# A new slot order for a six-layer transformer kernel, with five slots between projection and last use

## The chip, the cores and the metric

The kernel runs on one core of one Trainium2 chip. The metric is device time in microseconds (us) of one execution, taken as the median over runs. Everything is fp32 except the three-term projections, which use fp32r halves, and a bf16 mask.

## The reference

`x` is (8 batches, 256 tokens, 128 features). A layer norm comes first, and from its result two branches are computed:

```
s = linear_attention(xn) with a 3-tap convolution, then Wp, bp      # small, done once ahead of the layers
for i in range(6):                                                   # the bulk
    q, k, v = shift_tokens(x) @ Wqkv[i]          # 16 heads of 64
    q, k = l2norm(q) * qs, l2norm(k) * ks, then rotary with a scale
    att = softmax(8 * q k^T) v                   # windows of 32, each sees itself and the window before
    x = att @ Wo[i] + x
    h = layernorm(x) * g + b
    a, gate = shift_tokens(h) @ W1[i] + b1       # 341 + 341
    x = (a * gelu(gate)) @ W2[i] + b2 + x
out = x_in + s * silu(x)
```

## The kernel before

A step is one batch of one layer, so there are 6 x 8 = 48 steps, called n. A step has four units j = 0..3, one for each pair of a head octet and a 128-token tile; unit u = 4n + j. All five engines run one software pipeline written out by hand: each engine has a `body(n)` with a loop over four slots, and in slot u it works on unit u and on older units and older batches. Order within an engine is the order of the lines; engines meet only through semaphores.

What happens to a unit u, and in which slot, before the change:

- TensorE projects q, k, v of unit u into the PSUM banks ps_q, ps_k, ps_v (three matmuls each) in slot u.
- VectorE multiplies ps_q and ps_k with the rotary tables (`rotate`, two instructions each, into qk and qk_rot); ScalarE squares them (`squares_of`), VectorE sums the squares (`sum_squares`), clamps; ScalarE takes Ln and Exp (`start_norms`); VectorE does three small Newton instructions. GpSimd adds the rotary halves (`add_halves`) and multiplies by the norms (`normalise`). All in slot u.
- TensorE transposes q and k (`turn_qk`, into ps_qs and ps_tk) in slot u+2, ScalarE copies them out (`keep_turned`), TensorE computes the scores in the same slot (`scores`, 65 matmuls into ps_qs), VectorE finds and subtracts the maximum, ScalarE takes Exp, VectorE sums and inverts (`sums`).
- GpSimd divides (`divide`), TensorE transposes the probabilities (`turn_p`, into ps_po), ScalarE copies them block-diagonally (`keep_p`, two instructions), TensorE multiplies with v (`values`, 32 matmuls), ScalarE copies the result (`keep_attention`) in slot u+3.

The batch's own work hangs in certain slots: the out projection in two halves (`out_projection`), the layer norm (`ln_mean`, `ln_variance`, `ln_spread`), the first FFN matmul in three parts (`ff_up`, each copied by `ff_copy`), `gelu` on ScalarE, the gate product on GpSimd (`ff_gate`), the second FFN matmul (`ff_down`, 12 matmuls). Gelu needs another activation table than Ln and Exp, so ScalarE loads a table twice in each step. `ff_down` of batch n-3 is in slot j = 2 of step n, into ps_f.

Three rules of buffers matter. `qk` has two buffers, so `rotate(u)` waits until unit u-2 is transposed (`wait(dve, (tq_done, tk_done)[i], u - 1)`). `project(u+1)` waits until the bank ps_q (ps_k) of unit u is read. ps_po holds transposed probabilities, then the attention result, so `turn_p` waits for the `keep_attention` before it.

The pipeline is filled by running the first steps with what isn't there left out (`live`), steps from LAG on are a hardware loop, and `drain()` on each engine ends it, with silu and the last sums of the output.

Of the kernel before, what the change touches and what calls it, by code (L numbers as in the profile page):

```python
# [28 lines left out]
P = 128  # L29
# [10 lines left out]
UNITS = 4  # L40
STEPS = DEPTH * BATCHES
LAG = 3
# [20 lines left out]
def build(nc, x, wq, wk, wv, wp, bp, conv_w, conv_b, wqkv, q_scale, k_scale, wo, ln_g, ln_b, w1, b1, w2,  # L63
          rotary, masks, eye, head_block, out):
    with ExitStack() as ctx:
# [52 lines left out]
        x_mid = sb("x_mid", [P, 2, PADDED])  # L118
# [53 lines left out]
        silu_plain, silu_scaled, silu_inverted, silu_product = sem("silu_plain"), sem("silu_scaled"), sem("silu_inverted"), sem("silu_product")  # L172
# [29 lines left out]
        def normed(n, j):  # L202

            return live(UNITS * n + j) or (j == 1 and live_batch(n - 2))

        def norms_before(n, j):

            u = UNITS * n + j
            return u if live(u) else UNITS * STEPS + n - STEPS
# [28 lines left out]
        def middle(m, cols=slice(0, SHIFTED)):  # L238

            if isinstance(m, int) and m == STEPS - 1:  # L240
                return mid_last[:, cols]
            if isinstance(m, int):
                return x_mid[:, m % 2, cols]
            return x_mid[:, bass.ds(m % 2, 1), cols].rearrange("p a b -> p (a b)")
# [4 lines left out]
        def iterations(eng, body, last_layer_differs=False):  # L249

            for n in range(LAG):
                body(n)
            if last_layer_differs:
                with eng.Fori(LAG, (DEPTH - 1) * BATCHES) as n:
                    body(n)
                with eng.Fori((DEPTH - 1) * BATCHES, STEPS - 1) as n:
                    body(n, True)
                body(STEPS - 1)
            else:
                with eng.Fori(LAG, STEPS) as n:  # L260
                    body(n)


        silu_e = squares[:].rearrange("p a b -> p (a b)")
        END = UNITS * STEPS
        LAST = STEPS - 1
        spare = qk_rot[:].rearrange("p a b c -> p (a b c)")
        mid_last = table[:, ALL:ALL + PADDED]
        plain = table[:, 0:ALL]
        ff_a2 = spare[:, 0:FF_N * TOKENS].rearrange("p (a b) -> p a b", b=TOKENS)  # L270
        ff_g2 = spare[:, OCTET * 2:OCTET * 2 + FF_N * TOKENS].rearrange("p (a b) -> p a b", b=TOKENS)
# [5 lines left out]
        def _(sp):  # L277
# [56 lines left out]
            def body(n, b=3, l=0, slices=True):  # L334

                if slices:
                    load_slice(n + SLICES)
                for j in range(UNITS):
                    shift_v(n, j)
                    if b == 0 and j >= 2:  # L340
                        load_wo(l, j - 2)
                    if b == 2 and j == 0:
                        load_w1(l)
                    if b == 2 and j == 2:
                        load_w2(l)
# [5 lines left out]
            with sp.Fori(1, DEPTH - 1) as l:  # L351
                body(l * BATCHES, 0, l)
                body(l * BATCHES + 1, 1, l)
                body(l * BATCHES + 2, 2, l)
                with sp.Fori(3, BATCHES) as b:
                    body(l * BATCHES + b)
            n = (DEPTH - 1) * BATCHES
            body(n, 0, DEPTH - 1, slices=False)
            body(n + 1, 1, DEPTH - 1, slices=False)
            body(n + 2, 2, DEPTH - 1, slices=False)  # L360
            with sp.Fori(n + 3, STEPS) as n:
# [8 lines left out]
        def _(pool):  # L370
# [65 lines left out]
            def ff_gate(m):  # L436
                pool.wait_ge(gelu_done, m + 1)
                wait(pool, ff2_done, m)
                nc.gpsimd.tensor_tensor(ff_m[:, 0:FF_N - 1, 1:SHIFTED], ff_a[:, 0:FF_N - 1, :], ff_g[:, 0:FF_N - 1, :], ALU.mult)
                rows = slice(0, FF_ROWS[-1])  # L440
                nc.gpsimd.tensor_tensor(ff_m[rows, FF_N - 1, 1:SHIFTED], ff_a[rows, FF_N - 1, :], ff_g[rows, FF_N - 1, :],
                                        ALU.mult).then_inc(ff_mixed, 1)

# [17 lines left out]
            def body(n, last_layer=False):  # L461
                split = n < (DEPTH - 1) * BATCHES if isinstance(n, int) else not last_layer
                for j in range(UNITS):
                    u = UNITS * n + j
                    if live(u - 3):
                        divide(u - 3, (j - 3) % 2)
                    if live(u):
                        add_halves(u, j % 2)
                    if isinstance(n, int) and u == 0:
                        clear_edges()  # L470

                    if j == 1 and live_batch(n - 3):
                        ff_gate(n - 3)
# [5 lines left out]
                    if live(u):  # L479
                        normalise(u, j % 2)  # L480

            def silu_scale(b):

                c = columns(b)
                pool.wait_ge(silu_plain, b + 1)
                nc.gpsimd.tensor_tensor(s_out[:, c], s_out[:, c], plain[:, c], ALU.mult).then_inc(silu_scaled, 1)

            def silu_finish(b):
# [3 lines left out]
                nc.gpsimd.tensor_tensor(s_out[:, c], s_out[:, c], silu_e[:, c], ALU.mult).then_inc(silu_product, 1)  # L492
# [3 lines left out]
            def gate_spare(m):  # L496

                pool.wait_ge(gelu_done, m + 1)
                pool.wait_ge(ff2_done, m)
                nc.gpsimd.tensor_tensor(ff_m[:, 0:FF_N - 1, 1:SHIFTED], ff_a2[:, 0:FF_N - 1, :], ff_g2[:, 0:FF_N - 1, :], ALU.mult)  # L500
                rows = slice(0, FF_ROWS[-1])
                nc.gpsimd.tensor_tensor(ff_m[rows, FF_N - 1, 1:SHIFTED], ff_a2[rows, FF_N - 1, :], ff_g2[rows, FF_N - 1, :],
                                        ALU.mult).then_inc(ff_mixed, 1)

            def drain():
                divide(END - 3, 1)
                silu_scale(0)
                silu_scale(1)
                divide(END - 2, 0)
                divide(END - 1, 1)  # L510
                silu_scale(2)
                silu_finish(0)
                ff_gate(LAST - 2)
                silu_finish(1)
                silu_scale(3)
                silu_scale(4)
                gate_spare(LAST - 1)
                silu_finish(2)
                silu_scale(5)
# [14 lines left out]
        def _(pe):  # L534
# [101 lines left out]
            def turn_qk(u, i, s):  # L636

                ps, normed, read, done = ((ps_qs, q_normed, sub_done, tq_done), (ps_tk, k_normed, k_turned, tk_done))[i]
                wait(pe, read, u)
                pe.wait_ge(normed, u + 1)  # L640
# [87 lines left out]
            def ln_spread(n, m):  # L728

                pe.wait_ge(rnorm_done, norms_before(n, 1) + 1)  # L730
# [16 lines left out]
            def ff_up(m, i):  # L747
                rows = FF_ROWS[i]
                if i == 0:
                    wait(pe, x_ready, BATCHES + m)  # L750
                    pe.wait_ge(xn_ready, m + 1)
# [3 lines left out]
                mm(ps_f[0:rows, 0:TOKENS], w1_sb[:, P * i:P * i + rows], xn[:], True, True)  # L755
                mm(ps_f[0:rows, TOKENS:2 * TOKENS], w1_sb[:, FF + P * i:FF + P * i + rows], xn[:], True, True
                   ).then_inc(ff1_done, 1)

            def ff_down(m):
                pe.wait_ge(xn_ready, m + 2)  # L760
                down_into(ps_f, m)
# [12 lines left out]
            def body(n):  # L774
                for j in range(UNITS):
                    u = UNITS * n + j
                    for i, ps, free, done in ((0, ps_q, q_squared, q_done), (1, ps_k, k_squared, k_done)):
                        if live(u):
# [4 lines left out]
                        if i == 1 and j == 0 and live_batch(n - 2):  # L783
                            ln_mean(n - 2)
                        if i == 0 and j == 1 and live_batch(n - 2):
# [756 lines left out]
```

## Time and profile before

| | us |
|---|---|
| median of 3 runs (lowest, highest) | 1839.14 (1838.91, 1840.05) |
| the profiled execution's own time | 1847.78 |
| its span, first to last instruction | 1846.0 |
| TensorE matmul busy | 1697.0 (92%) |
| VectorE busy | 1422.5 (77%) |
| ScalarE busy | 1343.9 (73%) |
| GpSimd busy | 1307.7 (71%) |
| chain that ended last: TensorE, ScalarE, issue, VectorE | 69%, 11%, 10%, 8% |

Busy is the time in which at least one instruction of the engine runs; the rows below are from this one profiled execution, at positions in us from the span's start.

### The profile page before, as it was taken

How to read it: one execution, taken by the hardware profiler on the slowest of the kernel's cores; microseconds unless marked ns; L12 is line 12 of the kernel's file. 1: busy time of each engine (PE TensorE's matmuls, PEld its weight loads, DVE VectorE, ACT ScalarE, POOL GpSimd, SP SyncE). 2: the span in 40 equal slices, each digit the busy share in tenths (PEclk: the TensorE clock that was granted, in tenths of full speed). 3: DMA queues.
4: the chain of work that ended last, by engine and by line, in shares of the span. 5: the costliest groups of instructions: out<-in, count | busy, mean ns of one | idle time of the engine just before them, and what ended most of it. 6: DMA issues, size and time to landing. Idle time of an engine off the chain costs nothing.

```text
span 1846.0 us, 68784 instructions
## 1 busy us (share of the span) xinstructions
PE 1697.0 (92%) x26160; PEld 1292.7 (70%) x26160; DVE 1422.5 (77%) x3011; ACT 1343.9 (73%) x2663; POOL 1307.7 (71%) x1305
## 2 busy tenths in 40 slices
PE   6889999999999999999999999999999999999984
PEld 5667777777677777767777777777777777677763
DVE  4488777787887778788777777878778787787763
ACT  3367777777777777777777777777777777777764
POOL 5187777777777777777777777777777777776654
PEclk8799999999999999999999999999999999999986
DMA  5011101011110111111011111111101001100000
GB/s 161 10 36 40 32 28 34 29 41 43 35 30 28 34 40 42 35 31 30 28 46 41 33 34 28 30 34 48 37 28 34 28 26 41 36 26 24 26 21 23
DMA packets 41407, 66.14 MB, mean 36 GB/s; under 512 B 7072, under 2 KB 16032, under 8 KB 41376
## 3 DMA queue, kind: packets, MB, share of 16 engines
q1 hardware_dynamic: 40224, 65.38, 11.9%
q10 hardware_dynamic: 1152, 0.34, 0.1%
q8 instruction: 20, 0.33, 0.1%
q14 instruction: 11, 0.09, 0.0%
HBM read 20.61 MB, written 1.05 MB: 12 GB/s over the span
## 4 chain that ended last, share of the span: by engine, by line
PE 69%; ACT 11%; issue 10%; DVE 8%; POOL 2%; ACTq 1%; DMA 0%; POOLq 0%; DVEq 0%
PE ps_a L536 11%; PE ps_qs L536 10%; PE ps_f L536 10%; PE ps_po L536 8%; PE ps_q L536 7%; PE ps_k L536 5%; PE ps_v L536 5%; PE ps_po L651 4%; PE ps_qs L642 3%; PE ps_tk L642 3%; DVE ssq L1273 2%; ACT p_bd L940 2%; DVE prob L1310 2%; ACT L1008 2%; ACT squares L946 2%
## 5 line engine op out<-in xcount | busy, mean ns | idle before, releaser
L425 POOL TENSOR_TENSOR qk<-qk,rnorm 128x512 f32<-128x512 f32 x384 | 393.2, 1045 | 298.5 <-DVE rnorm L1300 298.5
L417 POOL TENSOR_TENSOR qk<-qk,qk_rot 128x512 f32<-128x512 f32 x384 | 483.8, 1276 | 118.0 <-DVE qk_rot L1267 118.0
L1273 DVE TENSOR_REDUCE ssq<-squares 128x8 f32<-128x512 f32 x384 | 257.9, 681 | 71.0 <-ACT squares L946 58.1
L940 ACT COPY p_bd<-ps_po 64x512 f32<-64x512 f32 x380 | 219.0, 576 | 24.9 <-PE ps_po L651 22.5
L432 POOL TENSOR_TENSOR prob<-prob,row_inv 128x512 f32<-128x512 f32 x192 | 200.2, 1043 | 41.8 <-DVE row_inv L1319 41.8
L1316 DVE TENSOR_REDUCE row_sum<-prob 128x8 f32<-128x512 f32 x192 | 131.7, 686 | 119.8 <-ACT prob L1047 119.2
L536 PEld LDWEIGHTS ps_qs<-k_t,q_t 64*32 64x32 f32 x12224 | 178.8, 107 | 56.9 <-issue 56.9
L536 PE MATMUL ps_qs<-k_t,q_t 64*32 64x64 f32 x12224 | 209.7, 218 | 0.0
L1047 ACT ACTIVATE prob<-prob 128x512 f32<-128x512 f32 x190 | 120.0, 632 | 110.3 <-DVE prob L1310 107.0
L536 PEld LDWEIGHTS ps_po<-p_bd,v_back 128*64 128x64 f32 x3056 | 162.4, 138 | 48.0 <-issue 31.5
L536 PE MATMUL ps_po<-p_bd,v_back 128*64 128x64 f32 x3056 | 193.4, 225 | 1.1 <-ACT p_bd L940 1.0
L536 PE MATMUL ps_po<-p_bd,v_own 128*64 128x64 f32 x3056 | 189.2, 222 | 0.0
L536 PE MATMUL ps_a<-attn_t,wo_sb 128*64 128x257 f32 x1536 | 188.7, 387 | 0.0
L940 ACT COPY k_t<-ps_tk 128x512 f32<-128x512 f32 x191 | 112.3, 588 | 85.5 <-PE ps_tk L642 80.7
L1265 DVE TENSOR_TENSOR qk<-ps_q,table 128x512 f32<-128x512 f32 x192 | 132.7, 691 | 40.8 <-issue 29.5
L536 PEld LDWEIGHTS ps_po<-p_bd,v_own 128*64 128x64 f32 x3056 | 155.4, 138 | 0.0
L536 PE MATMUL ps_f<-xn,w_sb 128*128 128x256 f32 (+1 forms) x556 | 150.5, 393 | 5.1
L946 ACT ACTIVATE squares<-ps_k 128x512 f32<-128x512 f32 x192 | 115.2, 600 | 54.5 <-DVE qk_rot L1267 53.3
L1265 DVE TENSOR_TENSOR qk<-ps_k,table 128x512 f32<-128x512 f32 x192 | 131.2, 684 | 28.1 <-PE ps_tk L642 28.0
L946 ACT ACTIVATE squares<-ps_q 128x512 f32<-128x512 f32 x192 | 115.8, 603 | 41.4 <-DVE qk_rot L1267 41.3
L651 PE MATMUL ps_po<-ident,prob 128*128 128x128 f32 x760 | 117.9, 277 | 29.8 <-POOL prob L432 29.8
L651 PEld LDWEIGHTS ps_po<-ident,prob 128*128 128x128 f32 x760 | 87.0, 140 | 80.4 <-issue 66.4
(231 smaller groups left out, 4102.3 us busy)
## 6 DMA issues: line engine op xcount, KB each, us to landing
v_back<-v_own SPq DMA_DIRECT2D x192, 192.0 KB, 2.4
w_raw<-in_wqkv SPq DMA_DIRECT2D x48, 192.0 KB, 2.3
v_back<-v_own SPq DMA_DIRECT2D x96, 64.0 KB, 2.1
wo_sb<-in_wo SPq DMA_DIRECT2D x12, 256.0 KB, 3.1
w_sb<-in_w SPq DMA_DIRECT2D x6, 341.0 KB, 3.4
w_sb<-in_w SPq DMA_DIRECT2D x6, 192.0 KB, 2.6
x_in<-in_x SPq DMA_DIRECT2D x4, 256.0 KB, 5.2
out<-s_out SPq DMA_DIRECT2D x8, 128.0 KB, 1.9
```

Source lines behind the costliest of these rows:

```text
L417: nc.gpsimd.tensor_tensor(qk[:, s, i, :], qk[:, s, i, :], qk_rot[:, s, i, :], ALU.add).then_inc(added, 1)
L425: nc.gpsimd.tensor_tensor(heads(qk[:, s, i, :]), heads(qk[:, s, i, :]), rnorm[:, s, 8 * i:8 * i + 8].unsqueeze(2).to_broadcast([P, 8, HEAD ...
L432: nc.gpsimd.tensor_tensor(heads(prob[:, s, :]), heads(prob[:, s, :]), row_inv[:, s, :].unsqueeze(2).to_broadcast([P, 8, HEAD]), ALU.mult). ...
L536: return nc.tensor.matmul(o, lhs, rhs, start=start, stop=stop, **kw)
L642: last = nc.tensor.transpose(ps[:, P * c:P * c + P], qk[:, s, i, P * c:P * c + P], ident[:])
L651: last = nc.tensor.transpose(ps[:, P * c:P * c + P], prob[:, s, P * c:P * c + P], ident[:])
L940: return nc.scalar.copy(o, i)
L946: nc.scalar.activation(squares[:, s, OCTET * i:OCTET * i + OCTET], (ps_q, ps_k)[i][:], ACT.Square).then_inc((q_squared, k_squared)[i], 1)
L1047: nc.scalar.activation(prob[:, j % 2, :], prob[:, j % 2, :], ACT.Exp, scale=QK_SCALE).then_inc(exp_done, 1)
L1265: V.tensor_tensor(heads(qk[:, s, i, :]), heads(ps[:]), cos.unsqueeze(1).to_broadcast([P, 8, HEAD]), ALU.mult)
L1273: V.tensor_reduce(ssq[:, s, 8 * i:8 * i + 8], heads(squares[:, s, OCTET * i:OCTET * i + OCTET]), AX, ALU.add).then_inc(ssq_done, 1)
L1316: V.tensor_reduce(row_sum[:, s, :], heads(prob[:, s, :]), AX, ALU.add).then_inc(sum_done, 1)
```

## The change

The five bodies get a new order, and LAG becomes 5. In slot u TensorE now does: q of u, the scores of u-3, the transposition of probabilities of u-4, k of u, v of u, then the batch's part (out projection, layer norm or FFN), then the transpositions of q and k of u-2, in slot 1 `ff_down` of batch n-4 into ps_tk, and at last the values of u-4. The batch's work is also spread otherwise (out projection halves in slots 3 and 0, `ff_up` in slots 1, 2, 3, of batch n-3). `ff_down` waits for the copy of the k that was just transposed into the same bank. Squares now come ahead of rotations, and `sums` too. On ScalarE the gelu and its table load close slot 0, and the load back is in slot 1. The drain is written anew, with two more sets of FFN buffers and three silu starts moved into the last step. Nothing of the mathematics changes.

```diff
-LAG = 3
+LAG = 5
 # TensorE, body(n)
-                    for i, ps, free, done in ((0, ps_q, q_squared, q_done), (1, ps_k, k_squared, k_done)):
-                        if live(u):
-                            project(n, j, i, ps, free, done)
-
-                        if live(u - 2):
-                            turn_qk(u - 2, i, j % 2)
...
+                    project(n, j, 0, ps_q, q_scaled, q_done)
+                    if live(u - 3):
+                        scores(u - 3, (j - 3) % UNITS, (j - 3) % 2)
+                    if live(u - 4):
+                        turn_p(u - 4, j % 2)
+                    project(n, j, 1, ps_k, k_scaled, k_done)
...
+                    project(n, j, 2, ps_v, v_copied, v_done)
+                    if j == 0:
+                            out_projection(n - 2, 1)
+                            ln_spread(n - 3, u)
+                    if j == 1:
+                            ln_mean(n - 2)
+                            ff_up(n - 3, 0)
+                    if j == 2:
+                            ln_variance(n - 2)
+                            ff_up(n - 3, 1)
+                    if j == 3:
+                            ff_up(n - 3, 2)
+                            out_projection(n - 1, 0)
                     if live(u - 2):
+                        turn_qk(u - 2, 0, j % 2)
+                        if j == 2 and live_batch(n - 4):
+                            pe.wait_ge(x_ready, BATCHES + n - 3)
+                        turn_qk(u - 2, 1, j % 2)
+                    if j == 1 and live_batch(n - 4):
+                        ff_down(u - 2, n - 4)
+                    if live(u - 4):
+                        values(u - 4, n - 1, j, j % 2)
+            def ff_down(u, m):
+
+                pe.wait_ge(k_turned, u + 1)
+                down_into(ps_tk, m)
 # ScalarE
-                act.wait_ge((q_scaled, k_scaled)[i], u + 1)
+                act.wait_ge((q_done, k_done)[i], u + 1)
...
+                    if live(u - 5):
+                        keep_attention(u - 5, *place(n, j, 5))
+                    if live(u - 1):
+                        keep_v(u - 1, *place(n, j, 1))
+                    squares_of(u, 0, j % 2)
+                    if j == 1 and live_batch(n - 4):
+                        load_exp()
+                    if live(u - 1):
+                        start_norms(u - 1, (j - 1) % 2)
+                    if j == 2 and live_batch(n - 2):
+                        ln_square(n - 2)
+                    if live(u - 4):
+                        keep_p(u - 4, j % 2)
+                    if live(u - 3):
+                        softmax_exp(u - 3, (j - 3) % 2)
+                    squares_of(u, 1, j % 2)
                     if live(u - 2):
+                        keep_turned_q(u - 2, j % 2)
+                        keep_turned_k(u - 2, (j - 2) % UNITS)
+                    if j >= 1 and live_batch(n - 3):
+                        ff_copy(n - 3, j - 1)
+                    if j == 0 and live_batch(n - 4):
+                        load_gelu()
+                        gelu(n - 4)
 # VectorE: rotate waits for the squares; body(n)
-                dve.wait_ge(done, u + 1)
+                dve.wait_ge(squared, u + 1)
...
+                    if live(u - 3):
+                        softmax_shift(u - 3, (j - 3) % 2)
+                    if live(u - 1):
+                        newton(u - 1, (j - 1) % 2, u - 2)
+                    sum_squares(u, 0, j % 2)
+                    if live(u - 3):
+                        sums(u - 3, (j - 3) % 2)
+                    rotate(n, j, 0)
+                    rotate(n, j, 1)
+                    sum_squares(u, 1, j % 2)
...
+                    clamp_unit(u, j % 2)
 # GpSimd, body(n): normalise one slot later, halves last
+                    if live(u - 1):
+                        normalise(u - 1, (j - 1) % 2)
+                    if live(u - 3):
+                        divide(u - 3, (j - 3) % 2)
+                    add_halves(u, j % 2)
 # GpSimd, drain(), part
                 divide(END - 3, 1)
                 silu_scale(0)
+                divide(END - 2, 0)
                 silu_scale(1)
-                divide(END - 2, 0)
                 divide(END - 1, 1)
...
                 silu_finish(3)
+                gate_of(*ff_pairs[3], LAST)
                 silu_scale(6)
                 silu_finish(4)
-                ff_gate(LAST)
```

## Rows read from the trace of the kernel before

**Rows 1.** Windows: fill, 44 equal steps, drain (stretch, length, busy by engine, clock).
```profile
72.39:208.55 136.16, 124.32 (x1857) 97.13 (x1856) 107.17 (x226) 84.96 (x174) 97.65 (x97) 0.94 0.11 31
208.55:1779.30 1570.75, 1489.25 (x23672) 1133.53 (x23671) 1253.64 (x2685) 1199.86 (x2376) 1158.06 (x1126) 1.00 0.11 34
1779.30:1846.00 66.70, 36.24 (x374) 24.96 (x370) 27.41 (x47) 33.77 (x71) 25.61 (x33) 0.70 0.06 21
```

**Rows 2.** Timeline of TensorE, the three waits of one step's slot 1.
```profile
1038.28 0.66 PE L642 MATMUL ps_qs<-ident,qk 128*128 128x128 f32 x4 [0.30 <-DVE prob L1310]
...
1041.79 0.63 PE L651 MATMUL ps_po<-ident,prob 128*128 128x128 f32 x4 [0.56 <-POOL prob L432]
1043.11 0.38 PE L536 MATMUL ps_qs<-mask_b,ident_b 128*128 128x512 bf16 x1 [0.69 <-ACT k_t L940]
```

**Rows 3.** Timeline of TensorE, slot 3 of the same step, and `ff_down`.
```profile
1015.31 1.52 PE L536 MATMUL ps_f<-ff_m,w_sb 128*64 128x257 f32 x12
...
1020.91 0.50 PE L536 MATMUL ps_q<-w_hi,xs_hi 128*128 x1
...
1022.16 1.03 PE L536 MATMUL ps_f<-xn,w_sb 128*128 128x256 f32 x4
1022.84 0.59 PE L536 MATMUL ps_k<-w_hi,xs_hi 128*128 x1
...
1023.73 0.60 PE L642 MATMUL ps_tk<-ident,qk 128*128 128x128 f32 x4
1024.08 0.48 PE L536 MATMUL ps_v<-w_hi,xs_hi 128*128 x1
...
1026.63 1.96 PE L536 MATMUL ps_a<-attn_t,wo_sb 128*64 128x257 f32 x16
1028.42 0.28 PE L536 MATMUL ps_po<-p_bd,v_back 128*64 128x64 f32 x4
...
1029.63 0.50 PE L536 MATMUL ps_q<-w_hi,xs_hi 128*128 x1
```

**Rows 4.** Timeline of ScalarE, both table loads without a wait between, and one copy.
```profile
1038.26 0.63 ACT L1047 ACTIVATE prob<-prob 128x512 f32<-128x512 f32 x1
...
1039.26 0.59 ACT L940 COPY attn_t<-ps_po 128x512 f32<-128x512 f32 x1
1039.87 1.28 ACT L1008 ACT_TABLE_LOAD   x1
1041.16 0.84 ACT L1008 ACTIVATE ff_g<-ff_g 128x768 f32<-128x768 f32 x1
...
1042.38 0.59 ACT L940 COPY k_t<-ps_tk 128x512 f32<-128x512 f32 x1
...
1045.01 1.28 ACT L1038 ACT_TABLE_LOAD   x1
1046.30 0.22 ACT L978 ACTIVATE ssq_ln<-ssq_c 128x18 f32<-128x18 f32 x1
1046.55 0.22 ACT L980 ACTIVATE rn<-ssq_ln 128x18 f32<-128x18 f32 x1
```

**Rows 5.** Timeline of VectorE: a k rotation held by the transposition.
```profile
1024.36 0.69 DVE L1265 TENSOR_TENSOR qk<-ps_k,table 128x512 f32<-128x512 f32 x1 [0.62 <-PE ps_tk L642]
1024.97 0.68 DVE L1267 TENSOR_TENSOR qk_rot<-ps_k,table 128x512 f32<-128x512 f32 x1
```

**Rows 6.** Timelines of GpSimd and ScalarE in the drain.
```profile
1793.51 0.73 POOL L486 TENSOR_TENSOR s_out<-s_out,table 128x256 f32<-128x256 f32 x1 [4.91 <-ACT table L1016]
1794.19 2.04 POOL L432 TENSOR_TENSOR prob<-prob,row_inv 128x512 f32<-128x512 f32 x2
...
1833.08 1.26 POOL L439 TENSOR_TENSOR ff_m<-ff_a,ff_g 128x512 f32<-128x512 f32 x1
...
1828.73 1.28 ACT L1139 ACT_TABLE_LOAD   x1
```

**Rows 7.** TensorE after a long wait, fill and drain, and the clock there.
```profile
100.41 0.66 PE L642 MATMUL ps_qs<-ident,qk 128*128 128x128 f32 x4 [2.74 <-DVE prob L1310]
...
1789.12 1.01 PE L536 MATMUL ps_a<-mean_w,lnt 128*128 128x1 f32 x4 [2.42 <-ACT lnt L992]
...
98.00:101.00 3.00, 0.59 (x5) 0.59 (x6) 2.80 (x7) 1.05 (x4) 2.50 (x4) 1.00 0.00 0
1789.00:1799.00 10.00, 6.62 (x52) 5.14 (x54) 4.36 (x12) 4.69 (x12) 2.73 (x3) 0.50 0.01 2
```

More of the change, by code:

```diff
@@ L200, in live_batch, with place @@
             return not isinstance(m, int) or 0 <= m < STEPS
[L202 to L209, printed above, removed]
+        def place(n, j, back):
+            return n + (j - back) // UNITS, (j - back) % UNITS
         def wait(eng, s, value):
@@ L832, in drain @@
+                pe.wait_ge(k_turned, c)
+                turn_into(ps_tk, c, 1, 0)
+                out_projection(LAST - 1, 1)
                 pe.wait_ge(k_scaled, END)
-                turn_into(ps_k, c, 0, 1)
+                turn_into(ps_k, d, 0, 1)
+                scores(c, 2, 0, ps_q)
                 pe.wait_ge(v_copied, END)
-                turn_into(ps_v, c, 1, 1)
+                turn_into(ps_v, d, 1, 1)
+                values(a, LAST, 0, 0)
+                ln_spread(LAST - 2, END)
@@ L849, in drain @@
-                ln_spread(STEPS, LAST - 1)
-                values(c, LAST, 3, 1, ps_tk)
-                up_into(ps_k, LAST - 1, 0)
-                pe.wait_ge(sub_done, b + 1)
+                pe.wait_ge(sub_done, b + 1)
+                scores(d, 3, 1, ps_qs)
+                ff_up(LAST - 2, 0)
+                pe.wait_ge(attn_copied, a + 1)
+                values(b, LAST, 1, 1)
+                ln_variance(LAST - 1)
+                ff_up(LAST - 2, 1)
+                turn_p(c, 0, ps_v)
+                ff_up(LAST - 2, 2)
@@ L853, in drain @@
+                values(c, LAST, 2, 0, ps_tk)
+                out_projection(LAST, 0)
+                turn_p(d, 1, ps_k)
+                ln_spread(LAST - 1, END + 1)
+                pe.wait_ge(sub_done, END)
+                up_into(ps_q, LAST - 1, 0)
                 up_into(ps_qs, LAST - 1, 1)
                 up_into(ps_f, LAST - 1, 2)
+                values(d, LAST, 3, 1)
+                down_into(ps_v, LAST - 3)
                 out_projection(LAST, 1)
-                pe.wait_ge(sub_done, END)
@@ L1056, in keep_p_from @@
-            def keep_p_from(ps, u, s):
-                act.wait_ge(pt_done, u + 1)
-                for h in range(2):
-                    rows = slice(64 * h, 64 * h + 64)
-                    last = copy(p_bd[rows, s, :, h, :], ps[rows, :].rearrange("p (g q) -> p g q", q=WINDOW))
-                last.then_inc(p_turned, 1)
-            def attention_from(ps, u, tile):
-                act.wait_ge(o_done, u + 1)
-                copy(attn_t[:, PAIRS:2 * PAIRS, 1 + P * tile:1 + P * tile + P],
-                     ps[:].rearrange("p (c t) -> p c t", t=P)).then_inc(attn_copied, 1)
```

529 lines of the change are left out of this document (210 added, 319 removed).

## The prediction

> **What bounds the kernel now.** I read the page first: TensorE is busy for 92% of the span, the three others for 71 to 77%, so TensorE's order decides. The windows cut the run into three parts [rows 1]: a fill of 136.16 us up to the end of step 3, then 44 steps in 1570.75 us, that is 35.70 us a step at the full clock (1.00, the 2.4 GHz level), then a drain of 66.70 us at a mean clock of 0.70. One full step in TensorE's timeline shows where it stands still. Nearly all of that is in slot 1: 0.30 us for the subtraction of the maximum, 0.56 us for the divided probabilities, 0.69 us for the copy of the transposed k [rows 2], 1.55 us in all. So a step has 35.70 - 1.55 = 34.15 us of matmul work with its small gaps. That is the floor of any order: the change can give at most 44 x 1.55 = 68 us in the steps. The reason for slot 1's waits is on ScalarE: two table loads of 1.28 us each and gelu stand ahead of copies that TensorE wants [rows 4]. VectorE works 1253.64 / 44 = 28.5 us a step, ScalarE 27.3, GpSimd 26.3 [rows 1]; none is full.
>
> **What the change removes.** Each of the three waits sat inside a round trip within one slot. Transposition, copy and scores are now a slot apart, division and `turn_p` too, and between the scores of u-3 and the transposition of q, which needs their bank, lie k, v and the batch's part. All three waits, 1.55 us, go.
>
> **What it adds in the step.** `ff_down` has a new wait: it writes ps_tk and so stands behind ScalarE's copy of the k transposed just before. In slot 1 that copy is late, because ScalarE's queue from the k copy of slot 0 to the k copy of slot 1 holds both table loads. I lay this ring out from rows. The same fourteen instructions stand once without a wait, from 1038.26 to 1046.55 plus some 0.25 for the last: 8.54 us [rows 4]. Around them: the first k copy starts about 0.7 us after the transposition starts (0.62 idle for a reader of the same bank, and q's copy ahead) [rows 5]; one more copy of 0.59; 0.12 for a load that can't overlap the instruction ahead; 0.14 from the copy's end (1042.97) to TensorE's start at 1043.11 [rows 2, 4]. Sum 10.1 us from k's transposition in slot 0 to `ff_down`. Everything else that ScalarE waits for there is early.
>
> TensorE's part meanwhile: slot 3 lasts 1029.63 - 1020.91 = 8.72 us; less one `ff_up` (1022.84 - 1022.16 = 0.68) and one half of the out projection (1028.42 - 1026.63 = 1.79) a unit alone is 6.25 us, of which the values are 1.2 and a transposition 0.35 [rows 3]. From the one transposition to the end of the next it has 6.25 + 0.35 + 0.68 + some 0.4 for `ln_mean` = 7.7 us. So TensorE loses 10.1 - 7.7 = 2.4 us a step there, in one piece or nearly. It is the cost of the change, and more than the 1.55 us it removes.
>
> The rest of the step from `ff_down` on, by the same rows: `ff_down` 1.5, values 1.1; slot 2: 6.25 + 0.68 + 0.4 (variance) = 7.33; slot 3: 8.72; slot 0 up to its k transposition: 6.25 - 1.2 - 0.35 + 1.79 + 0.4 (spread) = 6.89. Sum 25.54. Step: 10.1 + 25.54 = 35.64 us. The unit of 6.25 carries gaps of slot 3; where a block runs without them a unit is some 0.1 less, so 35.2 is the low end.
>
> **The rotations.** `rotate(u)` waits for the transposition of u-2, because of the two buffers; that now comes late in slot u, and q of u+1 waits for this rotation. VectorE starts some 0.65 us after the transposition's start and has two instructions, of which the second ends 0.61 + 0.68 = 1.29 later [rows 5]: 1.95 us with a handover. TensorE meanwhile has 0.4 + 0.35 + 1.2 = 1.95 us of work. This is just covered; I charge 0.1 us a step, with 0 and 0.4 (0.13 in three slots) as bounds. If cover is gone each microsecond counts in all slots but slot 1. VectorE itself needs 28.5 us of the 35.7, but its slot now begins at the scores and ends some 4.0 us behind q's transposition, 0.15 us before its next start. Taken: 35.75 us a step, 35.2 to 36.1. In 44 steps against 35.70: +2 us (-22 to +18).
>
> **A rule against the change.** Both table loads lie on the ring. Their rows show 1.28 us each, and the next instruction starts 0.01 us later (1039.87 + 1.28 to 1041.16) [rows 4]; so I charge 1.29. The Trainium skill, ScalarE: Activation LUTs, What ACT_TABLE_LOAD costs, adds a drain of about 1.38 us to each switch. By it the ring would be an estimated 2.8 us longer, and the step 38.4 us; the row speaks for no such drain here, and the sum goes by the row.
>
> **Queues moved past.** SP's stores of v now follow a copy one slot later; the values come three slots on, and a copy takes microseconds. The weights of W1, W2 and Wo are asked for in steps shifted by one like their users. GpSimd ends `add_halves` last in a slot, but its users are a slot off. I charge nothing; what hides them is a slot of 7 us or more.
>
> **Fill.** Before, the sixteen first slots take 136.2 us, hardly less than full ones, since the tight round trips idle TensorE there (2.74 us once) [rows 1, 7]. After, VectorE's 28.5 / 4 = 7.1 us bounds a slot until the batch's work has come in: slot 0 as before, 15.2; three slots without softmax at some 5.9; slots 4 to 11 at 7.1 to 8.0, 60 together; slots 12 to 15 at 34.15 less 1.5 (no `ff_down`), some 32. Sum 125: -11 us (-5 to -15).
>
> **Drain.** It gets one slot's work more, 7 to 8 us of TensorE. But before, the two last divisions stood behind a silu product that waited 4.91 us, and the last gate began at 1833.08 although gelu was done at 1828.7 [rows 6]; the new order takes both away, 3.3 and 4.4 us, and brings three silu starts into the last step. I laid out ScalarE's queue by its durations: last out projection done at about 28 us as before (28.1), last layer norm at 35 in place of 43. 56 us in place of 66.7: -10.5 (-3 to -14).
>
> **Sum.** 72.4 + 125 + 44 x 35.75 + 56 = 1826.4, against the span of 1846.0: -20 us. The profiled execution (1847.78) is longer than the median 1839.14, so the difference is applied to the median: 1819.
>
> **Rivals.**
> 1. *The new wait costs less.* If ScalarE got to the k copy in time, the step falls towards 34.15 us, 1819 - 44 x 1.6 = 1749; half way, 1784. For it: durations of ScalarE overlap. Against: the ring is a plain sum in a strict queue. Chance 0.14.
> 2. *Slower: the late rotation becomes the bound.* Place: q of the next slot behind `rotate`, behind q's transposition. If VectorE is not free at that moment, because sums or squares are late, TensorE waits in slots 0, 2 and 3. At 0.3 us in each the step is 36.65, total 1819 + 40 = 1859. It decides from 0.15 us a slot on: 0.46 us a step eats the 20 us of fill and drain. For it: VectorE's margin of 0.15 us. Against: in slots 0 and 3 the out projection gives 1.8 us more. Chance 0.22.
> 3. *The clock falls.* The new wait is 2 us in one piece, each step. After a wait of 2.42 us the drain ran ten us at 0.50 (1.2 GHz), after one of 2.74 us in the fill the clock stayed 1.00 [rows 7]. If it fell in each step for such a stretch, up to 5 us each, the time would be near 2000. The Trainium skill, TensorE: Matmul & The Clock Gate, HAM oscillation, describes such a fall repeated in every tile. The wait here is shorter than both rows and dense work surrounds it. Chance 0.03.
> 4. *No change.* Fill and drain gain 12 and the step costs 0.3 more: 1839. Chance 0.09.
>
> The likeliest, 0.52, is 1819, with its own range 1803 to 1835. A measurement of this kernel can tell 0.2%, 3.7 us. Faster: 0.52 + 0.14 = 0.66; same 0.09; slower 0.25. The range of 8 in 10 goes from rival 1's half-way point, 1784, to rival 2's 1857.
>
> **What would show it.** One step between 35.2 and 36.1 us; a wait of TensorE on ScalarE's k_t ahead of the 12 matmuls of `ff_down`, 2.0 to 2.4 us, once a step, some 44 times; none of the three old waits; step 4 starting at about 197 us; a drain of 53 to 62 us. I would be wrong if q projections wait on VectorE in every slot, if that k_t wait is under 1 us, or if the clock after it reads 0.5.

## The result: 3.6% slower

| | before | after |
|---|---|---|
| median of 4 runs each (lowest, highest), us | 1839.6 (1838.91, 1847.91) | 1907.4 (1906.47, 1914.47) |
| span of the profiled execution, us | 1846.0 | 1906.0 |

The ratio is 1.0363 (95% interval 1.0333 to 1.0392). The forecast was 1819, range 1784 to 1857: wrong in sign, and the time lies outside the range.

The windows of the changed kernel, cut as before's (columns: stretch, length, busy time and instructions of TensorE, its weight loads, VectorE, ScalarE and GpSimd, granted clock, DMA share, GB/s), show fill, 44 steps, drain:

```profile
66.00:196.26 130.26, 116.23 (x1702) 91.56 (x1714) 108.22 (x215) 76.77 (x162) 91.91 (x92) 0.92 0.12 33
196.26:1845.00 1648.74, 1524.91 (x23498) 1182.83 (x23673) 1314.28 (x2685) 1192.46 (x2384) 1162.75 (x1127) 0.96 0.11 32
1845.00:1906.00 61.00, 41.88 (x508) 28.83 (x510) 33.53 (x58) 36.22 (x76) 31.10 (x37) 0.83 0.07 23
```

Against [rows 1]: the 44 steps begin at 196.26 in place of 208.55, so everything ahead of them is 12.3 us shorter; the drain is 5.7 us shorter; the steps take 1648.74 in place of 1570.75, 78.0 us more. Sum +60.0, the whole difference of the spans. A step is 37.47 us in place of 35.70, and the clock of this stretch reads 0.96 in place of 1.00. That second number is half of the story.

The list of waits names one wait of TensorE that fills every step (engine, bank, line, releaser, us in total, times, longest), and of the three waits of [rows 2] none is left:

```profile
PE ps_tk L529 <- ACT k_t L937: 86.6, 44, 2.0
```

TensorE's timeline around it in one step (start, busy us, tile, shape, count, idle before):

```profile
1026.95 0.60 PE L639 MATMUL ps_tk<-ident,qk 128*128 128x128 f32 x4
...
1034.55 0.60 PE L639 MATMUL ps_tk<-ident,qk 128*128 128x128 f32 x4
1037.12 1.64 PE L529 MATMUL ps_tk<-ff_m,w_sb 128*64 128x257 f32 x12 [1.98 <-ACT k_t L937]
1040.40 0.80 PE L529 MATMUL ps_q<-w_hi,xs_hi 128*128 x1
...
1048.45 0.50 PE L529 MATMUL ps_q<-w_hi,xs_hi 128*128 x1
```

Read the last two rows together: the same q matmul takes 0.80 us at 1040.40 and 0.50 us one slot later. The windows give the clock of the stretch behind the wait, of the stretch ahead of it, and of a step in which nothing fell:

```profile
1038.50:1041.90 3.40, 3.40 (x37) 2.65 (x34) 2.35 (x5) 1.07 (x2) 3.14 (x4) 0.51 0.00 0
1023.50:1037.10 13.60, 11.42 (x154) 8.63 (x153) 10.79 (x25) 11.49 (x20) 10.26 (x10) 1.00 0.10 29
361.00:398.76 37.76, 33.33 (x535) 25.92 (x539) 31.43 (x65) 28.65 (x58) 28.29 (x28) 1.00 0.12 36
```

So while `ff_down` runs, behind the wait of 1.98 us, the clock falls to 1.2 GHz (0.51) for 3.4 us, and is then at 2.4 GHz again. It does so in 37 of the 44 steps. The distances between one `ff_down` and the next say what it costs: of the 43, the 37 behind a fall are around 37.73 us (all but the last one between 37.6 and 37.8), the other six between 36.0 and 36.1 (mean 36.1). The wait is 1.97 or 1.98 us in both kinds, only the first and the last are 1.84. A fall costs 1.6 us. All falls together: 1648.7 - 44 x 36.12 = 59.5 us (36.12 is the step without a fall, measured below). Without them the profiled span would be 1846.5, that of before.

The seven waits without a fall do not lie about at random. The starts of two falls in neighbouring steps are always 37.55 us apart, but the `ff_down`s are 37.73 apart, so each fall begins some 0.2 us earlier, seen from its `ff_down`, than the one before it. Here are three falls and a step that is spared; their `ff_down`s start at 398.76, 436.40, 662.86 and 700.64:

```profile
400.10:403.51 3.41, 3.41 (x37) 2.67 (x34) 2.38 (x5) 1.07 (x2) 3.15 (x4) 0.50 0.00 0
437.65:441.06 3.41, 3.41 (x39) 2.62 (x35) 2.48 (x5) 1.07 (x2) 3.15 (x4) 0.50 0.00 0
662.94:666.35 3.41, 3.41 (x30) 2.35 (x32) 3.38 (x7) 0.46 (x2) 3.15 (x4) 0.50 0.00 0
700.50:704.00 3.50, 3.35 (x47) 2.49 (x48) 3.47 (x7) 1.49 (x4) 3.23 (x4) 1.00 0.00 0
```

The fall begins 1.3 us after the start of `ff_down`, then a little less each time, down to 0.3 us or less; then one wait stays without a fall, the next step is 36.1 us, and the row starts again at 1.2 to 1.4. The first row of the run begins in the middle, at 0.6; the others are all like this, and so are those of e8_gate_late below (35 falls in 44 steps). So a wait of this length brings a fall or not by the moment at which it comes.

ScalarE's timeline shows what TensorE waits for:

```profile
1027.64 0.59 ACT L937 COPY k_t<-ps_tk 128x512 f32<-128x512 f32 x1
1028.25 1.28 ACT L1039 ACT_TABLE_LOAD   x1
1029.54 0.84 ACT L1019 ACTIVATE ff_g<-ff_g 128x768 f32<-128x768 f32 x1
...
1031.87 1.28 ACT L1042 ACT_TABLE_LOAD   x1
1033.16 0.22 ACT L981 ACTIVATE ssq_ln<-ssq_c 128x18 f32<-128x18 f32 x1
...
1036.33 0.60 ACT L937 COPY k_t<-ps_tk 128x512 f32<-128x512 f32 x1
```

Between the k copies of slots 0 and 1 nothing is idle: the ring from k's transposition in slot 0 (1026.95) to `ff_down` (1037.12) is 10.17 us.

### The profile page after: what moved, and what is told of

Its sections match the earlier page's. It is cut to its first block, busy times and chain, and to the rows that moved or that the text cites. A ratio compares the mean times of both kernels' runs of the same rounds, so it can differ in the third digit from the quotient of the medians.

```text
span 1906.0 us, 68566 instructions
## 1 busy us (share of the span) xinstructions
PE 1728.6 (91%) x25968; PEld 1339.4 (70%) x26160; DVE 1486.3 (78%) x3011; ACT 1330.8 (70%) x2661; POOL 1312.9 (69%) x1305
## 3 DMA queue, kind: packets, MB, share of 16 engines
HBM read 20.61 MB, written 1.05 MB: 11 GB/s over the span
## 4 chain that ended last, share of the span: by engine, by line
PE 84%; DVE 5%; issue 5%; ACT 4%; DVEq 1%; ACTq 0%; DMA 0%; POOL 0%; POOLq 0%
PE ps_a L529 12%; PE ps_qs L529 11%; PE ps_q L529 10%; PE ps_po L529 9%; PE ps_f L529 9%; PE ps_v L529 7%; PE ps_k L529 7%; PE ps_po L648 6%; PE ps_tk L529 5%; PE ps_qs L639 5%; PE ps_tk L639 3%; DVE qk_rot L1246 2%; ACT q_t L937 1%; ACT k_t L937 1%; DVE qk L1244 0%
## 5 line engine op out<-in xcount | busy, mean ns | idle before, releaser
L937 ACT COPY q_t<-ps_qs 128x512 f32<-128x512 f32 x190 | 111.0, 584 | 221.6 <-PE ps_qs L639 221.6
L937 ACT COPY p_bd<-ps_po 64x512 f32<-64x512 f32 x378 | 217.8, 576 | 29.8 <-PE ps_po L648 25.8
L529 PE MATMUL ps_po<-p_bd,v_back 128*64 128x64 f32 x3056 | 221.2, 243 | 0.0
L937 ACT COPY attn_t<-ps_po 128x512 f32<-128x512 f32 x191 | 113.2, 593 | 146.2 <-PE ps_po L529 146.2
L529 PE MATMUL ps_po<-p_bd,v_own 128*64 128x64 f32 x3056 | 213.2, 238 | 0.0
L1277 DVE TENSOR_REDUCE row_max<-ps_qs 128x8 f32<-128x512 f32 x191 | 130.3, 682 | 101.2 <-PE ps_qs L529 101.1
L529 PEld LDWEIGHTS ps_po<-p_bd,v_own 128*64 128x64 f32 x3056 | 175.9, 154 | 0.0
L529 PE MATMUL ps_tk<-ff_m,w_sb 128*64 128x257 f32 (+1 forms) x540 | 91.3, 485 | 86.6 <-ACT k_t L937 86.6
L1257 DVE TENSOR_SCALAR ssq_c<-ssq 128x18 f32<-128x18 f32 x194 | 157.8, 813 | 7.0
L529 PEld LDWEIGHTS ps_a<-attn_t,wo_sb 128*64 128x64 f32 x1536 | 101.3, 136 | 77.3 <-issue 34.3
L1280 DVE TENSOR_TENSOR prob<-ps_qs,row_max 128x512 f32<-128x512 f32 x191 | 132.1, 691 | 14.0
```

The lines of the kernel that those rows point to most:

```text
L529: return nc.tensor.matmul(o, lhs, rhs, start=start, stop=stop, **kw)
L937: return nc.scalar.copy(o, i)
L1257: V.tensor_scalar(ssq_c[:, s, :], ssq[:, s, :], 1e-24, SQ_SCALE, ALU.max, ALU.mult).then_inc(ssq_clamped, 1)
L1277: V.tensor_reduce(row_max[:, s, :], heads(ps[:]), AX, ALU.max).then_inc(max_done, 1)
L1280: V.tensor_tensor(heads(prob[:, s, :]), heads(ps[:]), row_max[:, s, :].unsqueeze(2).to_broadcast([P, 8, HEAD]), ALU.subtract).then_inc(sub ...
```

## Experiments

Times are medians; ratios are against the kernel before, on the same chip. "Step" is the distance between the same matmul of two steps in the middle of the run.

| run | us | ratio (95%) | step | main wait in a step |
|---|---|---|---|---|
| after | 1907.4 | 1.0363 (1.0333 to 1.0392) | 37.47 | `ff_down`, 1.98 |
| e1_fill6 | 1847.34 | 1.0023 (1.0009 to 1.0037) | 36.13 | the same, 1.33 |
| e1_fill16 | 1849.48 | 1.0036 (1.0020 to 1.0051) | 36.13 | the same, 0.24 |
| e2_values_first | 1807.99 | 0.9799 (0.9782 to 0.9815) | 35.19 | the same, 0.90 |
| e4_no_tables | 1800.5 | 0.9765 (0.9733 to 0.9797) | 35.00 | the same, 0.92 |
| e5_before_no_tables | 1785.94 | 0.9705 (0.9671 to 0.9739) | 34.55 | |
| e3_down_slot2 | 1846.31 | 1.0007 (0.9995 to 1.0019) | 36.08 | q on rotation, 1.5 |
| e6_rotate_first | 1853.71 | 1.0053 (1.0030 to 1.0076) | 36.18 | `turn_p` on division, 1.56 |
| e7_sums_late | 1832.71 | 0.9932 (0.9907 to 0.9956) | 35.70 | `turn_p` on division, 1.1 |
| e9_sums_between | 1808.36 | 0.9810 (0.9789 to 0.9830) | 35.34 | k's transposition on the sum behind `ff_down`, 0.5 |
| e10_after_q | 1846.34 | 1.0021 (1.0009 to 1.0034) | 36.06 | q on rotation, 1.53 |
| e11_both | 1807.05 | 0.9821 (0.9796 to 0.9845) | 35.30 | q on rotation, 0.72 |
| e8_gate_late | 1908.52 (one execution) | | 37.4 | `ff_down`, 1.98 |

**Is it the clock?** The wait stays, but TensorE does idle work in it: transposes of the identity into a free part of ps_a, ahead of the wait (the signal that ps_a is read by was moved behind them).

```diff
             def ff_down(u, m):
+                for _ in range(16):            # 6 in the other kernel
+                    last = nc.tensor.transpose(ps_a[:, 3 * P:4 * P], ident[:], ident[:])
+                last.then_inc(mean_done, 1)
                 pe.wait_ge(k_turned, u + 1)
```

> The kernel after, with sixteen transpositions of the identity (results unused) put between k's transposition and ff_down's wait in slot 1 of each full step. Theory A (ScalarE's ring sets the step at 36.1 us, and the idle stretch of 1.98 us lets TensorE's clock fall to half in 36 of 44 steps, at 1.6 us each): the wait shrinks to some 0.2 us, no fall, the step stays 36.1, total 1907 - 36 x 1.6 = 1850. Theory B (the fall has nothing to do with the idle stretch, or the step is bound by TensorE's own work): 1907 or up to 1907 + 44 x 1.8 = 1985.

> The same with six such transpositions, so that some 1.3 us of the idle stretch stay. Theory A with a fall that needs nearly the whole 2 us: 1850 as with sixteen. A fall that needs only a short gap: near 1907.

The waits in both, and one whole step of the kernel with 6:

```profile
PE ps_tk L529 <- ACT k_t L942: 10.0, 42, 0.2
```

```profile
PE ps_tk L529 <- ACT k_t L942: 58.2, 44, 1.3
```

```profile
1009.56:1045.68 36.12, 33.98 (x540) 26.56 (x545) 29.86 (x62) 27.03 (x55) 26.66 (x27) 1.00 0.14 41
```

The clock reads 1.00 in all steps of both kernels, and they take 58 to 60 us less than after, although they hold 44 x 6 and 44 x 16 instructions more. The place of `ff_down` is unmoved (step 36.12 with either), so the ring sets it; filler changes nothing but the clock. Six transposes do as much as sixteen: of the idle time 0.65 us less is enough. This shows the 60 us. Whether the transposes count as work for the clock or only make the idle stretch shorter, these two runs don't tell apart; the next one fills the stretch with work of the kernel's own, and has no fall in its steps either.

**Is the wait ScalarE's ring?** `ff_down` goes behind the values, so that TensorE has 1.1 us of work more before it needs the copy.

```diff
-                    if j == 1 and live_batch(n - 4):
-                        ff_down(u - 2, n - 4)
                     if live(u - 4):
                         values(u - 4, n - 1, j, j % 2)
+                    if j == 1 and live_batch(n - 4):
+                        ff_down(u - 2, n - 4)
```

> The kernel after, with ff_down of slot 1 behind the values in place of ahead of them. Theory A: ff_down still starts 10.1 us after slot 0's transposition of k, but 1.1 us of the wait is filled with values; wait 0.9 us, no fall, step 35.0, total 1907 - 36 x 1.6 - 44 x 1.1 = 1801. Theory B (the step is bound elsewhere, for example by rotations held by the late transposition): gain of the clock at most, 1850 or more.

```profile
1023.09 0.60 PE L639 MATMUL ps_tk<-ident,qk 128*128 128x128 f32 x4
1025.68 1.52 PE L529 MATMUL ps_tk<-ff_m,w_sb 128*64 128x257 f32 x12 [0.90 <-ACT k_t L937]
```

Two lines swapped turn 3.6% slower into 2.0% faster: 99 us, of which some 60 are the falls and 44 x (36.12 - 35.19) = 41 the hidden part of the wait. What is left, 0.90 us, is the ring again: 1.98 - 1.1 of values = 0.88.

**The table loads.** Both kernels without loads; Square stands in for Gelu, so gelu isn't computed.

```diff
-                nc.scalar.preload_act_table_set("gelu_and_others")
+                pass
...
-                nc.scalar.preload_act_table_set("natural_log_exp_and_others")
+                pass
-    ACT.Gelu
+    ACT.Square
```

> The kernel after with Square in place of Gelu and no table loads behind the first; this leaves gelu out. Theory A (ring of ScalarE with both loads): the ring shortens by 2.6 us to 7.5, under TensorE's 7.7, so ff_down waits 0 to 0.3 us, no fall of the clock, step 34.1 to 34.4, total 1765 to 1780. If the wait of ff_down came from the round trip of the k copy itself, some 0.8 us would stay: 1800.

> The kernel before with the same left out (Square in place of Gelu, no loads behind the first). If the three waits of slot 1 (1.55 us) come from the table loads, they shrink to about 0.3 us: 1840 - 44 x 1.25 = 1785. If they come from the round trips within a slot, most stay: 1820 or more.

Before gains 1.15 us a step and lands on the expected 1785, but not in the expected way. Of the three waits of slot 1 only the one on k's copy is gone (0.69 us, 31.6 in all before). The two others, said to shrink with it, stand as they did, 0.57 and 0.28 us a step (29.8 and 16.8 in all before):

```profile
PE ps_po L651 <- POOL prob L432: 28.7, 49, 1.0
PE ps_qs L642 <- DVE prob L1310: 16.7, 47, 2.7
```

So the table loads made one of the three waits, and the prediction's reading that the reason for all of them is on ScalarE is wrong for the other two; that the total fits is luck. A wait also costs more than its idle time: from the start of `turn_p` to the start of the scores it is 1.32 us with the wait of 0.69 [rows 2] and 0.46 without, so the wait cost 0.86, since matmuls that don't wait overlap a little. The rest of the gain is in pieces of under 0.2 us.

After gains 1.12 us a step plus the falls, and keeps a wait, now the bare round trip from k's transposition through the copy to `ff_down`, with nothing of TensorE's between:

```profile
PE ps_tk L529 <- ACT k_t L937: 40.2, 44, 0.9
```

By idle time alone, 35.00 - 0.92 = 34.08, the new order without any stall would be near the 34.15 us that the prediction named as the floor. It isn't a floor of any order: before without loads takes 34.55 us with 0.85 us of waits still in it. And with the loads gone the old order is the better one, 1785.94 against 1800.5.

**Can `ff_down` be put where nothing waits?** First in slot 2's batch part, its sum on VectorE just ahead of slot 2's rotations:

```diff
                     if j == 2:
+                        if live_batch(n - 4):
+                            ff_down(u - 3, n - 4)
...
                         sums(u - 3, (j - 3) % 2)
+                    if j == 2 and live_batch(n - 4):
+                        after_ff(n - 4)
                     rotate(n, j, 0)
```

> The kernel after, with ff_down at the start of slot 2's batch part, where the k copy it needs is long done, and after_ff on VectorE just ahead of slot 2's rotations. Theory A: no wait of ff_down, no fall, step 36.1 less 2.0 = 34.1, total 1907 - 36 x 1.6 - 44 x 2.0 = 1762, faster than both. Theory B (late rotations become the bound once the wait is gone): step 34.7 or more, 1790 and up.

`ff_down` waits for nothing now, and the step is 36.08 all the same. The wait has moved to q of slot 2; the timeline of all engines at the end of slot 1:

```profile
474.40 0.63 ACT L976 ACTIVATE prob<-prob 128x512 f32<-128x512 f32 x1
475.06 0.69 DVE L1286 TENSOR_REDUCE row_sum<-prob 128x8 f32<-128x512 f32 x1 [0.51 <-ACT prob L976]
475.78 0.20 DVE L1289 RECIPROCAL row_inv<-row_sum 128x8 f32<-128x8 f32 x1
476.00 0.69 DVE L1244 TENSOR_TENSOR qk<-ps_q,table 128x512 f32<-128x512 f32 x1
...
477.44 0.49 PE L529 MATMUL ps_q<-w_hi,xs_hi 128*128 x1 [1.52 <-DVE qk_rot L1246]
```

This is the other half of the change, "sums ahead of rotations". Exp is late in slot 1: ScalarE works without a pause from the first of the two table loads up to it. VectorE waits for it (0.51), then sums, and only then rotates what TensorE's q bank waits for. In the changed kernel the same wait of 0.51 us is there, hidden under the `ff_down` wait. (This order was not run without the loads.) Three orders of slot 1 on VectorE, each with `ff_down` as in this kernel:

```diff
 # e6_rotate_first: rotate q, newton, rotate k, sums
 # e7_sums_late: newton, rotate q, rotate k, sums
 # e9_sums_between: newton, rotate q, sums, rotate k
-                    if live(u - 3):
+                    if j != 1 and live(u - 3):
                         sums(u - 3, (j - 3) % 2)
...
                     rotate(n, j, 0)
+                    if j == 1 and live(u - 3):
+                        sums(u - 3, (j - 3) % 2)
                     rotate(n, j, 1)
```

> The run with ff_down in slot 2, and on VectorE in slot 1 the rotation of q ahead of newton, and sums behind both rotations, so that neither the late norms nor the late Exp of ScalarE holds q of the next slot. Theory A2 (the ring of ScalarE came back through Exp, sums, rotation and q's projection, 1.53 us a step): this wait goes, step 34.1 to 34.6, total 1846 - 44 x 1.6 = 1775, faster than both kernels. Theory B2 (VectorE's own amount of work or the two qk buffers bound the step): 1820 or more.

> The same run with only sums put behind both rotations in slot 1; newton stays ahead. Theory A2: q's rotation now starts behind the norms, some 1.5 us earlier than behind sums, so the wait of q falls from 1.53 to 0.1 us or none: 1780. If it is newton that is late: 1820.

> ff_down in slot 2, and in slot 1 on VectorE newton, the rotation of q, then sums, then the rotation of k. In e7 the transposition of the probabilities waited 1.1 us a step for GpSimd's division, because sums came last; here sums ends some 1.2 us earlier, so the division is done before TensorE asks, while the rotation of q still goes ahead of it. If these two are the whole of what ScalarE's lateness costs, step 34.1 to 34.5, total 1832.7 - 44 x 1.2 to 1.6 = 1762 to 1780, 3 to 4% faster than before. If another wait takes their place, 1800 or more.

The first two give q what it wants and make the probabilities late. In the first, the small Newton steps come later, so GpSimd starts two normalisations late, and the division stands behind them in its queue:

```profile
510.10 2.04 POOL L426 TENSOR_TENSOR qk<-qk,rnorm 128x512 f32<-128x512 f32 x2 [3.59 <-DVE rnorm L1272]
...
512.26 1.04 POOL L433 TENSOR_TENSOR prob<-prob,row_inv 128x512 f32<-128x512 f32 x1
...
513.44 0.63 PE L648 MATMUL ps_po<-ident,prob 128*128 128x128 f32 x4 [1.56 <-POOL prob L433]
```

In the second the sums alone are late (1.1 us of wait). Only the sums between the two rotations serve both users, but the 1762 to 1780 expected of this did not come: 1808.36. The next wait is again one on VectorE, which adds `ff_down`'s result out of ps_tk before k may be transposed into it. The timelines of GpSimd, VectorE and TensorE in slot 2 of a middle step, and VectorE at the same place of a late one:

```profile
933.64 1.00 POOL L406 TENSOR_TENSOR w_lo<-w_raw,w_hi  x1 [0.26 <-POOL w_hi L403]
933.71 0.96 DVE L1272 SCALAR_TENSOR_TENSOR rnorm<-rn_b,rn 128x18 f32<-128x18 f32 x1
936.77 0.66 PE L639 MATMUL ps_tk<-ident,qk 128*128 128x128 f32 x4 [0.51 <-DVE x_run L1318]
...
1603.19 0.18 DVE L1272 SCALAR_TENSOR_TENSOR rnorm<-rn_b,rn 128x18 f32<-128x18 f32 x1
```

The third Newton instruction takes 0.96 us beside GpSimd's `w_lo`, the splitting of weights for the next layer. It is so once in each of 36 steps. In the six steps after them GpSimd has no weights left to split, the instruction takes 0.18 us, the wait is gone and the step is 34.58 us in place of 35.35. That the one instruction stretches the other is read from this and was not tested by a run.

**The same at another place.** `ff_down` right behind q of slot 2, whose 1.2 us should cover the 0.90 us left by the kernel with the values first; its sum behind slot 2's Newton steps. The second kernel has the sums between the rotations as well.

```diff
                     project(n, j, 0, ps_q, q_scaled, q_done)
+                    if j == 2 and live_batch(n - 4):
+                        ff_down(u - 3, n - 4)
```

> The second FFN matmul goes into slot 2, right behind the q projection, a place between the values of slot 1 (where it waited 0.90 us and the step took 35.2 us) and the batch's part of slot 2 (where it waited for nothing, but the sum behind it made the k transposition late, and with the probabilities' sums ahead of the rotations the step took 36.1 us). Its sum on VectorE follows the norms' small steps of slot 2. Theory A: q's 1.2 us cover the 0.90 us that were left of the wait, and nothing else is late: a step of 34.3 us, 1770 us. Theory B: ScalarE's lateness from its two table loads reaches q of slot 2 through exponential, sums and rotation anyway: 35.5 to 36 us, 1820 to 1845 us. No fall of the clock in the steps by either.

> As the kernel before it in this list, with slot 1's sums of the probabilities between the rotation of q and that of k. Theory A: the same 1770 us, since the sums were not late. Theory B: the way from exponential through sums to q is cut, so 0.5 to 1 us a step less than without it, some 1790 to 1808 us.

```profile
430.83 0.50 PE L529 MATMUL ps_q<-w_hi,xs_hi 128*128 x1 [1.53 <-DVE qk_rot L1246]
```

```profile
433.67 0.68 DVE L1286 TENSOR_REDUCE row_sum<-prob 128x8 f32<-128x512 f32 x1
...
434.50 0.68 DVE L1244 TENSOR_TENSOR qk<-ps_q,table 128x512 f32<-128x512 f32 x1
...
435.83 0.50 PE L529 MATMUL ps_q<-w_hi,xs_hi 128*128 x1 [0.72 <-DVE qk_rot L1246]
```

Theory B holds in both. In the second kernel slot 1 is free, and what is left is the same pattern a slot later: in slot 2 the sums still stand ahead of q's rotation, and q of slot 3 waits 0.72 us. The kernels with the values first, with the sums between, and with both changes end within 1.3 us of one another; they are the fastest here that compute gelu, 1.8 to 2.0% under before. In the kernel with both changes a Newton instruction is long in the same 36 steps (0.84 us), and in the six after them the 0.72 us are gone too, at 34.61 us a step; the one with the values first keeps its 35.2 us to the end, as ScalarE's ring sets it.

**The drain.** After's last gate was moved behind one scaling and one finish of silu, as in before's order.

> The kernel after with the last gate of the drain put back behind two silu products, as the kernel before has it. If the last gate's place gave the 4.4 us of the forecast, this drain is some 4 us longer than after's 61.0; if gelu or silu itself decided, no change.

One execution, 1908.52 us. Timelines of ScalarE, GpSimd and TensorE around the last gate, first after, then this kernel:

```profile
1893.19 0.84 ACT L1019 ACTIVATE ff_g<-ff_g 128x768 f32<-128x768 f32 x1
1894.11 1.26 POOL L440 TENSOR_TENSOR ff_m<-ff_a,ff_g 128x512 f32<-128x512 f32 x1 [3.18 <-ACT ff_g L1019]
```

```profile
1889.36 0.84 ACT L1019 ACTIVATE ff_g<-ff_g 128x768 f32<-128x768 f32 x1
1894.62 1.26 POOL L440 TENSOR_TENSOR ff_m<-ff_a,ff_g 128x512 f32<-128x512 f32 x1
1896.61 1.98 PE L529 MATMUL ps_f<-ff_m,w_sb 128*64 128x257 f32 x8 [8.95 <-POOL ff_m L442]
```

From gelu's end to `ff_down` it is 6.41 us here (1890.20 to 1896.61) and 2.08 in after, where `ff_down` starts at 1896.11. The 4.33 us between them are the 4.4 us that the prediction gave to the gate. The starts of `ff_down` differ by 0.5 us only because this execution had two falls less and came to its drain earlier: from the last `ff_down` of the steps to the end it is 83.6 us here and 79.9 in after, 3.7 more.

## Why the prediction was wrong

**The step that failed: the wait was priced at its own length.** The prediction had the wait's place, its cause and its size, "2.4 us a step" (1.98 measured, 44 times), and counted it as idle time alone. What the wait does to the clock stood as rival 3 with a chance of 0.03, because "the wait here is shorter than both rows and dense work surrounds it". Both were true and neither protected: 37 waits of 1.98 us brought the clock to the 1.2 GHz level, the waits of 1.56 us (e6), 1.5 (e3, e10), 1.33 and 0.90 us in the experiments never. The two rows it was judged by [rows 7] were one case each, and they already contradicted each other (fall after 2.42 us, none after 2.74), so they could not carry a chance that small. The rival's size was too large, "up to 5 us each": a fall here cost 1.6 us, because 3.4 us of work ran at half the clock. The Trainium skill, TensorE: Matmul & The Clock Gate, HAM oscillation, describes the pattern, a fall in each tile behind a wait for a transfer of some 3 to 5 us. The trace agrees with the pattern, and here waits of 1.98 us were enough.

The falls aren't the whole miss. With the clock held (e1_fill6) the kernel is at 1.0023 of before, where 1819 would have been 0.989: the rest is in the step, in the drain and in the offset below.

The account in spans, forecast 1826.4, measured 1906.0:

| term | forecast | measured | difference |
|---|---|---|---|
| start of the 44 steps | 197.4 | 196.3 | -1 |
| step without a fall, x 44 | 35.75 | 36.12 | +16 |
| falls of the clock | 0 | 59.5 | +60 |
| drain | 56 | 61.0 | +5 |

The sum is 80. From there to the medians: the forecast took 8.6 us off since before's profiled execution was that much over the median, and after's was 0.4 over its own. So the offset was the scatter of one execution and no constant; it made the forecast 8 us worse.

**Three waits go:** right; none of them is in after's list. **The new wait on k's copy:** right in place and count. The ring is 10.17 us where 10.1 were laid out from rows. TensorE's own part was 10.17 - 1.98 = 8.2 us in place of 7.7, so the wait was 0.4 shorter; as the ring sets the step, this changed nothing.

**The rest of the step** was 25.95 us where 25.54 were summed. The timeline of e1_fill6, at the full clock throughout, cuts it:

```profile
1009.56 1.52 PE L529 MATMUL ps_tk<-ff_m,w_sb 128*64 128x257 f32 x12 [1.32 <-ACT k_t L942]
...
1011.95 0.50 PE L529 MATMUL ps_q<-w_hi,xs_hi 128*128 x1
...
1019.34 0.50 PE L529 MATMUL ps_q<-w_hi,xs_hi 128*128 x1
...
1023.38 1.02 PE L529 MATMUL ps_f<-xn,w_sb 128*85 128x256 f32 x4
1024.34 1.96 PE L529 MATMUL ps_a<-attn_t,wo_sb 128*64 128x257 f32 x16
...
1028.50 0.49 PE L529 MATMUL ps_q<-w_hi,xs_hi 128*128 x1
...
1035.51 0.60 PE L639 MATMUL ps_tk<-ident,qk 128*128 128x128 f32 x4
1045.68 1.52 PE L529 MATMUL ps_tk<-ff_m,w_sb 128*64 128x257 f32 x12 [1.33 <-ACT k_t L942]
```

`ff_down` and values 2.39 (2.6 taken), slot 2 7.39 (7.33), slot 3 9.16 (8.72), slot 0 up to k 7.01 (6.89). The miss is slot 3; 0.28 of its 0.44 is `ff_up`, 0.96 us from its start to the next matmul, where the row taken for it gave 0.68 with a k projection behind it [rows 3]. That row was the shortest of the three in its own step: the two others, ahead of the values, took 1.05 us (from 1018.78) and 1.03 (from 1034.90). Why the same four matmuls take longer there no run tells.

**Rotations:** the wait of q on them that was charged with 0.1 us is not in after's steps (nothing over 0.05 us). Rival 2's mechanism was real and was covered: as soon as the `ff_down` wait was gone, q waited 1.5 us in e3 and e10, once a step, from a cause the prediction hadn't named (the sums behind a late Exp). It was looked for behind the transposition, and it came from the other side of VectorE's queue.

**The rule against the change:** the load at 1028.25 takes 1.28 us and gelu starts at 1029.54, 0.01 later, and likewise 1031.87 and 1033.16; it is within 0.03 us for 90 of the 93 loads of the changed kernel. So the drain of 1.38 us per switch, which the Trainium skill adds under ScalarE: Activation LUTs, What ACT_TABLE_LOAD costs, isn't seen in after either, and the ring of 10.17 has no room for two of them.

**Fill** 12.3 us shorter, 11 forecast. **Drain** 5.7 shorter, 10.5 forecast: the gate's 4.4 came; but the last out projection was done 33.9 us after the drain's start, forecast 28, and the last layer norm at 42.2, forecast 35. In the layout of ScalarE's queue the batch's work was placed too early; which item of it is not settled.

**What stays open.** Why the falls keep a spacing of their own, and why waits of 1.98 us brought them and waits of 1.56 us, which stood at other places of the step, did not. And where the last half microsecond of the new order goes, 34.6 us in steps with no wait over 0.3 us against the 34.1 of the sum above; it is in small pieces.

## What to carry to other kernels

A wait on the engine that sets the pace has two prices: its length, and what the clock does after it. If an order makes one wait of 2 us out of three of half a microsecond, the sum of the waits is the wrong thing to compare: look whether the granted clock stays at 1.00, and split or fill the wait if it doesn't. And when a queue carries a fixed delay (here two table loads of 1.28 us), moving one user of it only shows the next user: list all who stand behind it, in order of time, before the order is changed.

## What the runs showed of the hardware

- Idle stretches of 1.98 us once a step, with TensorE's matmuls close together on either side, took the granted clock from 1.00 to 0.50 in 37 of 44 cases, for 3.4 us each, at a cost of 1.6 us each (in a second kernel with the same steps, e8_gate_late, in 35 of 44). Stretches of 1.5 us (e3_down_slot2, e6_rotate_first, e10_after_q, 42 times each), 1.33 us (44 times) and 0.90 us (44 times) never did.
- The starts of these falls were 37.55 us apart, or 75.1 over a spared step, while the waits were 37.73 us apart; whether a wait was spared went by when it came.
- Transposes of the identity, six in 2 us, were enough to keep the clock at 1.00; their own cost was nil, as the time was idle. Work of the kernel in their place (e2_values_first) kept it there too.
- The half clock lengthened the q matmul from 0.50 to 0.80 us where it reached it, and `ff_down`'s twelve from 1.52 to between 1.57 and 2.84, the longer the sooner the fall began after their start.
- After a table load of 1.28 us the next instruction of ScalarE started within 0.03 us, for 90 of the 93 loads of the changed kernel.
- A VectorE instruction on 128x18 elements that took 0.18 us alone took 0.96 us beside a GpSimd subtraction of 1.00 us, in 36 steps of e9_sums_between; in the changed kernel, where it fell beside a maximum out of PSUM (5 times), that kept its 0.7 us.
